# A block quantizer on VectorE: one masking step replaced by a sign product, reciprocals seeded in an integer tile, and the gate and up weights quantized 512 instead of 1024 columns at a time

## What is computed

```python
def _mx_dequant(t):
    blocks = t.reshape(rows, feat // 32, 32)
    max_abs = jnp.max(jnp.abs(blocks), axis=-1)
    scales = jnp.maximum(max_abs / 448.0, 1e-30)
    q = (blocks / scales[..., None]).astype(float8_e4m3fn).astype(float32)
    return (q * scales[..., None]).reshape(rows, feat)
def _mx_linear(x2d, w):
    return _mx_dequant(x2d) @ _mx_dequant(w).T
x = _layernorm(x + attention(x, w_qkv) @ w_o)        # x: (4, 4096, 2048)
h = silu(_mx_linear(x, gate_w)) * _mx_linear(x, up_w)  # gate_w, up_w: (8192, 2048)
out = _layernorm(x + _mx_linear(h, down_w))            # down_w: (2048, 8192)
```

## Time and profile before

| what | value |
|---|---|
| median of 2 runs | 54334.33 us (54194.45 to 54474.21) |
| the profiled execution | 54298.51 us, span of its slowest core (core 1) 54297.0 us |
| spans of the cores | die 0 (cores 0 to 3): 54154.8 to 54297.0 us; die 1 (cores 4 to 7): 53631.4 to 53860.2 us; medians 54197.5 and 53757.2 us |
| mean granted TensorE clock | 0.652 on core 1; 0.653 die 0, 0.659 die 1 (medians) |
| busy on core 1 | TensorE matmul 27714.6 us, VectorE 16207.3 us, ScalarE 4971.9 us, GpSimd 977.0 us |
| from the first weight quantization to the last, core 1 | 21560.6 to 38776.0 us (`p4w` reductions) |

### The profile page before, as it was taken

The page is one execution under the profiler, slowest core; times in us unless marked ns, Lnnn a source line. Parts: engine busy times, 40 slices in busy tenths (PEclk is TensorE's granted clock), DMA queues, the critical chain, the costliest instruction groups (busy, mean ns, idle before and its releaser), DMA issues.

```text
span 54297.0 us, 311521 instructions; the slowest of 8 cores (53631.4 to 54297.0 us)
## 1 busy us (share of the span) xinstructions
PE 27714.6 (51%) x69120; PEld 13029.2 (24%) x69120; DVE 16207.3 (30%) x33272; ACT 4971.9 (9%) x12826; POOL 977.0 (2%) x1828
## 2 busy tenths in 40 slices
PE   9999555555555561222222222222366666666665
PEld 5555222222222220110111001111122222222222
DVE  0000000000000006666666666566422222222222
ACT  0000222222222200000000000000000000000000
POOL 0000000000000001000000000000000000000000
PEclk8999555555555575555555555555677777777887
DMA  2222000000000020000000000000111111111111
GB/s 60 63 63 62 16 9 6 10 5 10 9 6 10 2 81 37 25 25 19 25 25 25 22 22 25 25 21 22 37 40 37 40 47 37 37 40 48 42 47 44
DMA packets 1010510, 1664.82 MB, mean 31 GB/s; under 512 B 129968, under 2 KB 588976, under 8 KB 945328
## 3 DMA queue, kind: packets, MB, share of 16 engines
q1 hardware_dynamic: 905904, 1292.45, 7.0%
q0 software_dynamic: 102912, 352.44, 1.7%
HBM read 1292.04 MB, written 352.32 MB: 30 GB/s over the span
## 4 chain that ended last, share of the span: by engine, by line
issue 32%; PEld 21%; DVE 16%; DVEq 12%; PEldq 11%; ACT 3%; DMA 2%; SPq 2%; ACTq 0%; POOLq 0%; POOL 0%
PEld ps L189 21%; DVEq L189 12%; DVE p4q_i L189 8%; PEldq L220 8%; DVE p4q_f L189 2%; SPq L198 2%; ACT p2P L189 2%; PEldq L208 2%; PEldq L221 2%; DVE stats L189 2%; DVE p4q_m L189 1%; DVE p4q_rs L189 1%; DMA p4t<-gqT 1%; DMA p4t<-uqT 1%; DVE p4w L189 0%
## 5 line engine op out<-in xcount | busy, mean ns | idle before, releaser
L189 PE MATMUL ps<-p4t,p4x 128*128 128x512 f32 x16384 | 8291.2, 671 | 1783.4 <-DMA p4t<-gqT 930.6
L189 PE MATMUL ps<-idt,p4w 128*128 128x128 f32 x3072 | 1373.5, 447 | 11702.1 <-DVEq L221 10672.1
L189 PEld LDWEIGHTS ps<-p4t,p4x 128*128 128x128 f32 x16384 | 3459.6, 214 | 6596.7 <-issue 6596.7
L189 PE MATMUL ps<-p4t,p4ht 128*128 128x512 f32 x8192 | 4304.1, 674 | 387.1 <-issue 334.1
L189 PE MATMUL ps<-p2pt,p2V 128*128 128x128 f32 x8704 | 3335.9, 487 | 1526.0 <-issue 1524.2
L189 PE MATMUL ps<-idt,p2P 128*128 128x128 f32 x3840 | 1718.7, 448 | 4152.3 <-DVEq L221 2935.9
L189 PEld LDWEIGHTS ps<-idt,p4w 128*128 128x128 f32 x3072 | 561.7, 183 | 12531.8 <-issue 12531.8
L189 DVE TENSOR_REDUCE stats<-p2S 128x1 f32<-128x256 f32 (+14 forms) x240 | 548.7, 2286 | 9783.7 <-ACTq L221 9783.7
L189 DVE TENSOR_TENSOR p4q_i<-p4q_i 128x512 f32<-128x512 f32 (+1 forms) x3840 | 3166.6, 866 | 147.6 <-issue 6.0
L189 DVE TENSOR_TENSOR p4b<-ps,p4h 128x512 f32<-128x512 f32 x256 | 177.1, 692 | 9486.0 <-PEq L221 9486.0
L189 PEld LDWEIGHTS ps<-p2pt,p2V 128*128 128x128 f32 x8704 | 2181.1, 311 | 2678.4 <-issue 2678.4
(11 more groups left out here) (107 smaller groups left out, 19105.4 us busy)
## 6 DMA issues: line engine op xcount, KB each, us to landing
p1w<-wqkv SPq DMA_DIRECT2D x3072, 64.0 KB, 2.1
p4t<-gqT SPq DMA_DIRECT2D x768, 256.0 KB, 5.2
p4t<-uqT SPq DMA_DIRECT2D x768, 256.0 KB, 5.2
p4t<-dqT SPq DMA_DIRECT2D x192, 1024.0 KB, 8.2
p3w<-wo SPq DMA_DIRECT2D x256, 256.0 KB, 6.1
p4w<-gw SPq DMA_DIRECT2D x64, 1024.0 KB, 9.0
gqT<-p4t POOLq DMA_DIRECT2D x256, 256.0 KB, 3.7
p4w<-uw SPq DMA_DIRECT2D x64, 1024.0 KB, 8.0
```

Source lines behind the costliest of these rows:

```text
L189: getattr(e, name)(*a, **k)
```

## The change

Five edits. (1) In the quantizer the seed of the reciprocal is worked out in an integer view of `i0` and then copied to `rs` by a multiplication by 1.0: one more narrow step. (2) The scaled value stays signed; its sign is made into a factor of plus or minus 1.0 by one TENSOR_SCALAR with two bit operations, the value is made positive by one product with it, and the sign is given back at the end by a second product. This takes the place of the mask with 0x7FFFFFFF, the mask of x's sign bit and the bitwise or. The wide steps are then 13 with two tensor inputs and 9 TENSOR_SCALAR, 22 as before. (3) The compare of each threshold writes into the output tile (the weights, rows or product themselves) instead of scratch `i1`, and the running value lives in a new scratch tile `f2`. (4) `emit_nr_recip` gets an integer tile and one more instruction with its drain. (5) Gate and up weights are quantized by eight calls on two tiles of 512 columns instead of four calls on two tiles of 1024, and the scratch tiles of `_build_p4` are sized for 512.

```diff
@@ emit_nr_recip
+    v.tensor_scalar(ti, ti, 8, None, op0=ALU.logical_shift_left)
+    v.drain()
+    v.tensor_scalar(out, ti.bitcast(F32), 1.0, None, op0=ALU.mult)
     v.drain()
@@ emit_quant
+    ii = [i0[i][:, 0:NB] for i in range(n)]
...
+        v.tensor_scalar(ii[i], ii[i], 8, None, op0=ALU.logical_shift_left)
+    guard()
+    for i in range(n):
+        v.tensor_scalar(rs[i], ii[i].bitcast(F32), 1.0, None, op0=ALU.mult)
     guard()
...
+    f2 = [scr['f2'][:, i * W:(i + 1) * W] for i in range(n)]
     for i, (x, _) in enumerate(tiles):
-        v.tensor_tensor(b3(i0[i].bitcast(F32)), b3(x), bc(rs[i]), op=ALU.mult)
-    guard()
-    for i in range(n):
-        v.tensor_scalar(i0[i], i0[i], 0x7FFFFFFF, None, op0=ALU.bitwise_and)
+        v.tensor_tensor(b3(f0[i]), b3(x), bc(rs[i]), op=ALU.mult)
...
+        v.tensor_scalar(i0[i], f0[i].bitcast(I32), -2147483648, 0x3F800000,
+                        op0=ALU.bitwise_and, op1=ALU.bitwise_or)
+    guard()
+    for i in range(n):
+        v.tensor_tensor(f0[i], f0[i], i0[i].bitcast(F32), op=ALU.mult)
...
     for Tth in (8.0, 4.0, 2.0, 1.0, 1.0):
-        for i in range(n):
-            v.tensor_scalar(i1[i].bitcast(F32), i0[i].bitcast(F32), Tth, -Tth,
-                            op0=ALU.is_ge, op1=ALU.mult)
+        for i, (_, o) in enumerate(tiles):
+            v.tensor_scalar(o, f2[i], Tth, -Tth, op0=ALU.is_ge, op1=ALU.mult)
         guard()
-        for i in range(n):
-            v.tensor_tensor(i0[i].bitcast(F32), i0[i].bitcast(F32),
-                            i1[i].bitcast(F32), op=ALU.add)
+        for i, (_, o) in enumerate(tiles):
+            v.tensor_tensor(f2[i], f2[i], o, op=ALU.add)
...
-    for i, (x, _) in enumerate(tiles):
-        v.tensor_scalar(i1[i], x.bitcast(I32), -2147483648, None,
-                        op0=ALU.bitwise_and)
-    guard()
-    for i in range(n):
-        v.tensor_tensor(i0[i], f1[i].bitcast(I32), i1[i], op=ALU.bitwise_or)
+    for i in range(n):
+        v.tensor_tensor(f0[i], f0[i], i0[i].bitcast(F32), op=ALU.mult)
     guard()
@@ _build_p4
-        scr = quant_scratch(nc, es, "p4q", 1024, 2)
+        scr = quant_scratch(nc, es, "p4q", 512, 2)
...
-                        for cl in range(4):
-                            tiles = [(wsl[:, (2 * cl + j) * 1024:
-                                          (2 * cl + j + 1) * 1024],) * 2
+                        for cl in range(8):
+                            tiles = [(wsl[:, (2 * cl + j) * 512:
+                                          (2 * cl + j + 1) * 512],) * 2
                                      for j in range(2)]
```

More of the change, by code:

```diff
@@ L18, with emit_nr_recip @@
 NTILE = OWN // 128
-def emit_nr_recip(v, out, in_, tmp, iters=3):
+def emit_nr_recip(v, out, in_, tmp, ti, iters=3):
     MAG = 0x7EF127EA >> 8
-    v.tensor_scalar(tmp.bitcast(I32), in_.bitcast(I32), 8, None,
+    v.tensor_scalar(ti, in_.bitcast(I32), 8, None,
                     op0=ALU.logical_shift_right)
     v.drain()
-    v.tensor_scalar(tmp.bitcast(I32), tmp.bitcast(I32), -1, MAG,
-                    op0=ALU.mult, op1=ALU.add)
+    v.tensor_scalar(ti, ti, -1, MAG, op0=ALU.mult, op1=ALU.add)
     v.drain()
-    v.tensor_scalar(out.bitcast(I32), tmp.bitcast(I32), 8, None,
-                    op0=ALU.logical_shift_left)
+    v.tensor_scalar(ti, ti, 8, None, op0=ALU.logical_shift_left)
+    v.drain()
+    v.tensor_scalar(out, ti.bitcast(F32), 1.0, None, op0=ALU.mult)
     v.drain()
@@ L76, in emit_quant @@
     for i in range(n):
-        v.tensor_scalar(rs[i].bitcast(I32), rs[i].bitcast(I32), -1, MAG,
-                        op0=ALU.mult, op1=ALU.add)
+        v.tensor_scalar(ii[i], ii[i], -1, MAG, op0=ALU.mult, op1=ALU.add)
     guard()
     for i in range(n):
-        v.tensor_scalar(rs[i].bitcast(I32), rs[i].bitcast(I32), 8, None,
-                        op0=ALU.logical_shift_left)
+        v.tensor_scalar(ii[i], ii[i], 8, None, op0=ALU.logical_shift_left)
+    guard()
+    for i in range(n):
+        v.tensor_scalar(rs[i], ii[i].bitcast(F32), 1.0, None, op0=ALU.mult)
     guard()
@@ L107, in emit_quant @@
     for i in range(n):
-        v.scalar_tensor_tensor(f1[i], f0[i], 0.5, i0[i].bitcast(F32),
+        v.tensor_scalar(i0[i], f0[i].bitcast(I32), -2147483648, 0x3F800000,
[3 more added lines that the diff above has]
+        v.tensor_tensor(f0[i], f0[i], i0[i].bitcast(F32), op=ALU.mult)
+    guard()
+    for i in range(n):
+        v.scalar_tensor_tensor(f0[i], f1[i], 0.5, f0[i],
                                op0=ALU.mult, op1=ALU.add)
@@ L111, in emit_quant @@
     for i in range(n):
-        v.tensor_scalar(i1[i], f0[i].bitcast(I32), -1, 254 << 23,
+        v.tensor_scalar(i1[i], f1[i].bitcast(I32), -1, 254 << 23,
                         op0=ALU.mult, op1=ALU.add)
@@ L154, in quant_scratch @@
         'f1': es.enter_context(nc.sbuf_tensor(name + "_f1", [128, n * wmax], F32)),
+        'f2': es.enter_context(nc.sbuf_tensor(name + "_f2", [128, n * wmax], F32)),
     }
@@ L303, in build @@
         S.wait("vector", "sldA", t2)
-        emit_nr_recip(V, r448[:], cons[:, 0:1], nrtmp[:])
-        emit_nr_recip(V, rn[:], cons[:, 2:3], nrtmp[:])
+        emit_nr_recip(V, r448[:], cons[:, 0:1], nrtmp[:], nri[:])
+        emit_nr_recip(V, rn[:], cons[:, 2:3], nrtmp[:], nri[:])
         S.pub("vector", "vv")
@@ L316, in build @@
         if nph >= 3:
-            _build_p3a(nc, S, es0, aT, wo, xo, x1d, cons, rn, nrtmp, ps)
+            _build_p3a(nc, S, es0, aT, wo, xo, x1d, cons, rn, nrtmp, nri, ps)
             S.barrier()
@@ L662, in _build_p2, with emit_ln @@
             head_pe_mark[hp] = last_pe
-def emit_ln(S, x_ap, out_ap, stats, ceps, sqscr, col0=16):
+def emit_ln(S, x_ap, out_ap, stats, ceps, sqscr, nri, col0=16):
     V = EngProxy(S, "vector")
@@ L690, in emit_ln @@
     S.wait("vector", "aa", aam)
-    emit_nr_recip(V, rstd, vart, tmp)
+    emit_nr_recip(V, rstd, vart, tmp, nri)
     S.op("vector", "tensor_tensor", nbt, mt, rstd, op=ALU.mult)
@@ L699, in emit_ln, with _build_p3a @@
     return S.pub("scalar", "aa")
-def _build_p3a(nc, S, es0, aT, wo, xo, x1d, cons, rn, nrtmp, ps):
+def _build_p3a(nc, S, es0, aT, wo, xo, x1d, cons, rn, nrtmp, nri, ps):
     import contextlib
@@ L829, in _build_p4 @@
 def _build_p4(nc, S, es0, x1qT, gw, uw, dw, gqT, uqT, dqT, x1d, out_d,
-              cons, rn, r448, nrtmp, idt, ps):
+              cons, rn, r448, nrtmp, nri, idt, ps):
     import contextlib
```

23 lines of the change are left out of this document (12 added, 11 removed).

## The result

| | before | after |
|---|---|---|
| median of all executions | 54,751.66 us (10; 54,086.53 to 55,428.8) | 56,960.11 us (11 timed; 56,119.79 to 57,267.94) |
| the profiled execution | 54,298.51 us | 56,496.87 us |
| VectorE instructions | 33,272 | 43,818 |
| VectorE busy | 16,207.3 us | 17,722.3 us |

The changed kernel is slower: ratio 1.036, 95% interval [1.029, 1.043]. The forecast had the direction and the ratio (1.034 over the profiled execution), but the time, 56,150 us with a range to 56,500, lies 810 us under the median. Five of the eleven timed executions of after (56,995 to 57,268 us) had one die over 1% behind the other at a lower granted clock, and the ratio leaves such executions out on both sides; the other six took 56,120 to 56,960 us.

A forecast was written before the change was run, and what follows sets the result against it. The prediction took the quantizer, standing bare while engines take turns, to bound the kernel. It added 1,674 + 223 + 20 + 7 = 1,924 us to 54,298.5, took 70 off for the clock, and gave 56,150 us, range 55,850 to 56,500.

The forecast's parts named there:

- What bounds the kernel: First row group, and product calls in later ones: engines take turns, so every microsecond of quantization lengthens the span.
- What a call costs: Gate and up quantizer calls: halving to 512 columns repeats 154 to 158 ns per instruction; slab 254.3 us, width 1,452 us.
- the rival of the hidden fixed part: Gate and up quantization: instruction overlap hides the 154 ns, so splitting costs nothing; 54,770 us, +0.9%, chance 0.02.
- Steps: Each quantizer call: one wide step becomes a two-input product and one narrow step is added; 0.87 us at 512 columns.
- the bound of 1,352 us for the compare: Quantizer in `_build_p4`: compares writing the output tile slow from 424 to 688 ns; at most 1,352 us there, chance 0.05.
- that of 270 us for the bit operations: Quantizer's new two-bit-operation instruction: takes between 424 and 688 ns, at most 270 us more; 56,420 us, inside the range.
- VectorE's busy time: Whole kernel: VectorE's busy time grows by nearly the same 1.9 ms as the span.
- The whole sum: Whole kernel: 1,674 gate and up, 223 product and down, 20 `_build_p3b`, 7 layer norms; 1,924 us in all.
- TensorE's clock: Matmuls of `rq` 0: longer pauses make fewer cores' matmuls coincide, giving back 70 us, between -148 and +283.
- the rival in which the clock pays the change back: Matmuls of `rq` 1 to 3 also speed up to 607 and 626 ns; 54,780 us, 0.9% slower, chance 0.03.
- The stretch of the earlier trace: In `rq` 1 to 3: clock 0.81 while cores 0 and 2 quantized and core 3 ran matmuls beside core 1.
- The range: Whole time: 55,850 to 56,500 us, from the clock's ends and, below, 220 us for run differences and clock gain.

The follow-up runs named there:

- with zeros: Kernels before and after with a tile of zeros as stationary operand of the projection, output projection and feed-forward matmuls: 52,646.25 us before, 54,604.98 us after.
- the width alone: Kernel before with only gate and up weights quantized in eight calls on 512 columns: ratio 1.026 with real operands; 54,087.53 us with zero stationary tile.
- three live cores: Kernel before with zeros for x on cores 3 and 7 only, three cores per die keeping real rows: 53,197 to 54,438 us.
- two live cores: Kernel before with zeros for x on cores 2, 3, 6 and 7, two cores per die keeping real rows: 52,752 to 52,963 us.

## Why the prediction was right and wrong

- **What bounds the kernel: right.** The wait of TensorE for VectorE grew by 1,924 us, in the same 376 waits (1,927 us with zeros).
- **What a call costs: right.** 254.55 us a slab for 254.3. The 154 ns that do not scale with the columns are paid by each instruction; the width alone costs 1,441 us for 1,452, and the rival of the hidden fixed part fell with it.
- **Steps: right.** 439 us for 432. The new forms run at the rates of their kind, so the bound of 1,352 us for the compare and that of 270 us for the bit operations came to nothing.
- **VectorE's busy time: wrong.** It was to grow by nearly the same 1.9 ms as the span and grew by 1,515 us, because the idle stretches between the steps are on the path too.
- **The whole sum: right within 2%,** 1,959 us for 1,924, both with zeros. The waits for loads in `rq` 1 to 3, which it put at nothing, took 33 us. By the 60 ns of the Trainium skill's table ("VectorE: DVE Perf Modes", section on the TRN2 errata) it would have been some 1,020, an estimate; the measured one decides for the rows. The same section says below its table that this row is too low and puts the fixed term at about 150 cycles, some 156 ns at the 0.96 GHz that it gives, which agrees with the 154 to 158 ns of the rows; the prediction took only the table from it.
- **TensorE's clock: the step that failed.** I took -70 us for it, between -148 and +283, on top of the level of one execution, and argued that longer pauses let fewer matmuls coincide. No run shows that gain: the four means rose by 6 to 19 ns, and the rival in which the clock pays the change back, with 607 and 626 ns in `rq` 1 to 3, fell against 689 and 690. In the profiled executions the loss by the clock was 54,298.5 - 52,646 = 1,652 us before and 56,496.9 - 54,605 = 1,892 after: +240, nearly all of the 274 us that the profiled execution lies above the sum. And between executions of one kernel the loss goes from 1,440 to 2,783 us before and from 1,515 to 2,663 after. My terms were thus worked out for stages of one execution, while the quantity is drawn anew in each. The 810 us between forecast and median are 35 us of the sum and some 773 us of this: the median loss of the kernel after is 2,355 us where I had 1,652 - 70 = 1,582. The profiled execution of after, with 56,496.9 us, lies just inside the range; which execution is looked at decides that.
- **The stretch of the earlier trace rows was misread.** I took 0.81 on core 1 and 0.84 on core 3 as one level that the two share. In steps of 20 us core 1 has 0.81 in each from 40080 to 40140 us, but core 3 has 0.53, 1.00 and 1.00: its 0.84 is a mean of half and full speed. The profile counts each core's time from that core's own first instruction, so equal times on two cores need not be the same moment, and that cores 0 and 2 were quantizing meanwhile, or that 0.81 came with two of the four cores at matmuls, is not shown.
- **The range: too narrow for the same reason.** I widened it below by 220 us, for two executions that differ by 280, and above not at all beyond the clock's 283. The next eight of before reached from 54,087 to 55,429 us; a level known from two executions is not known to 1%. Even 1.3% up from 56,150 us ends at 56,880, under the measured median; what comes near it is the ratio on the median of all ten executions of before, 54,751.66 x 1.034 = 56,613 us, 0.6% too low.
- **Whether the change itself raises the loss stays open.** Medians say 2,355 after and 2,105 before, but the ranges lie on each other, and the argument on coincidence was not tested by a kernel of its own; that a die's cores do not always share a level speaks against its simple form.

## What to carry to other kernels

A stage in which engines take turns can be priced to a few per cent from the trace alone: durations by form times counts, taken from a neighbouring stage that already has the new shape. Halving a tile of a many-step elementwise chain that stands bare on the path costs the fixed part of every instruction once more, here 154 ns of 688; the engine's busy time shows less than that (1,515 us where the path grew by 1,959), since the idle stretches between steps grow too. If all cores run dense float32 matmuls, as here, state a forecast as a ratio and give the level the spread of many executions; to measure an effect under 2%, repeat both kernels with zeros as the stationary operand, where executions differ by under 0.07%, and keep the real operands for the final time.

## What the runs showed of the hardware

- The values of the operands move the time of this kernel by 2.7 to 5.3%: 52,646 us with zeros against 54,087 to 55,429 with real ones, at the same instructions but for the one that writes the zeros.
- The lowered clock does not go by a core's own operands: with three live cores on the die, core 3, which multiplied by zeros, took 635 ns for a 128x512 float32 matmul, like its live neighbour core 0, and 618 with two live. It is not always shared by the whole die: on the other one cores 4 and 5 took 637 and 635 ns, cores 6 (live) and 7 (zeros) 614 and 613.
- Core 0 had a median of 592 ns with two live cores of four and of 698 with four; the first matmuls after a pause took up to 1,194.
- A VectorE instruction on float32 had a fixed part of 154 ns (two tensor inputs) or 158 (TENSOR_SCALAR) beside what goes with its columns, and a compare, a sign mask with two bit operations or a multiplication all took 423 or 424 ns at 512 columns.
- Adding and subtracting 1.5 x 2^20 times a value's own power of two took two steps of 688 ns at 512 columns, in place of the ten steps of the threshold loop; a quantizer call on 1024 columns went from 50.5 to 19.9 us.
